# Two pre-norm attention layers on one core: another order for the first four and the last two phases

## The reference

```python
h = jnp.maximum(_layernorm(x, axis=-1), 0.0)
x = x + _L0_gnn_ref(h, adj, ...)   # q, k, v = h @ W + b per head
    # scores = q k^T / sqrt(32) + beta * adj; masked where adj <= 0; softmax; @ v
h = jnp.maximum(_layernorm(x, axis=-1), 0.0)
x = x + _L1_gnn_ref(h, adj, ...)   # q, k = h @ Wq.T, h @ Wk.T; v = h @ Wv.T + bv
    # a = q k^T * 384**-0.5 + adj; softmax; (a v) @ Wo.T + bo
return x
```

## Time and profile before

| | |
|---|---|
| median of 3 runs | 2226.38 us (2223.99 to 2227.64) |
| profiled execution | 2224.74 us |
| its span | 2222.9 us |
| granted TensorE clock, mean | 0.996 |
| PE busy | 97% of the span |
| ACT busy | 92% |
| DVE, POOL busy | 82%, 69% |

### The profile page before, as it was taken

The page is one execution under the profiler, slowest core; times in us unless marked ns, Lnnn a source line. Parts: engine busy times, 40 slices in busy tenths (PEclk is TensorE's granted clock), DMA queues, the critical chain, the costliest instruction groups (busy, mean ns, idle before and its releaser), DMA issues.

```text
span 2222.9 us, 75547 instructions
## 1 busy us (share of the span) xinstructions
PE 2160.5 (97%) x19968; PEld 1422.3 (64%) x19968; DVE 1820.4 (82%) x10186; ACT 2045.3 (92%) x7816; POOL 1530.5 (69%) x2439
## 2 busy tenths in 40 slices
PE   4999999999999999999999999999999999999997
PEld 1666666666666666665666666666666666666665
DVE  4788888888888888887888888888888888888777
ACT  3999999999999999998999999999999999999987
POOL 4567766767667767667676677676676776676665
PEclk9999999999999999999999999999999999999999
DMA  9787767778577677676676776676767867777861
GB/s 222 131 134 145 126 137 141 134 134 159 123 140 138 132 148 136 136 143 123 135 159 120 140 142 130 148 135 137 143 132 134 156 128 135 143 134 129 141 107 48
DMA packets 461311, 303.36 MB, mean 136 GB/s; under 512 B 228432, under 2 KB 460880, under 8 KB 460880
## 3 DMA queue, kind: packets, MB, share of 16 engines
q1 hardware_dynamic: 460880, 298.45, 70.8%
HBM read 71.83 MB, written 25.17 MB: 44 GB/s over the span
## 4 chain that ended last, share of the span: by engine, by line
PE 85%; DVE 7%; issue 3%; ACT 2%; POOL 1%; DMA 1%; SPq 0%; DVEq 0%; POOLq 0%; ACTq 0%
PE job_bank L909 47%; PE pt_bank L932 13%; PE o_bank L945 8%; PE score_bank L922 7%; PE inv_bank L968 3%; PE post_bank L978 2%; PE post_bank L982 2%; PE post_bank L979 2%; PE post_bank L960 2%; DVE neg L712 2%; ACT probs L606 1%; DVE part_lo L780 1%; DVE inv_wide L772 1%; DMA h<-h_rows 1%; DVE off_zero L763 1%
## 5 line engine op out<-in xcount | busy, mean ns | idle before, releaser
L606 ACT ACTIVATE probs<-neg,neg_max 128x128 f32<-128x128 f32 x3072 | 1189.7, 394 | 50.7 <-DVE neg_max L712 50.7
L909 PE MATMUL job_bank<-h,w_hi 128*128 128x512 f16 x2304 | 725.4, 381 | 29.6 <-DMA h<-h_rows 27.0
L606 ACT ACTIVATION_READ_ACCUMULATOR probs<-neg,neg_max 128x1 f32 x3072 | 595.2, 194 | 0.0
L631 ACT ACTIVATE probs_t<-pt_bank 128x512 f32<-128x512 f32 x768 | 450.0, 586 | 32.4 <-PE pt_bank L932 29.5
L932 PE MATMUL pt_bank<-ident,probs 128*128 128x128 f32 x3072 | 463.8, 274 | 10.8 <-ACT probs_t L631 10.0
L909 PE MATMUL job_bank<-h,w_lo 128*128 128x512 f16 x1152 | 438.2, 380 | 0.0
L932 PEld LDWEIGHTS pt_bank<-ident,probs 128*128 128x128 f32 x3072 | 366.0, 141 | 93.7 <-issue 13.1
L544 POOL TENSOR_TENSOR pair_sum<-neg 128x256 f32<-128x256 f32 x384 | 280.9, 732 | 197.7 <-DVE neg_max L712 183.6
L909 PE MATMUL job_bank<-w_hi,h 128*128 128x384 f16 x1536 | 413.6, 326 | 1.3 <-DVE part_lo L780 0.9
L712 DVE CUSTOM_DVE_ANT_0 neg<-score_bank,bias 128x128 f32<-128x128 f32 x1536 | 354.0, 286 | 28.5 <-issue 26.5
L712 DVE CUSTOM_DVE_ANT_0 neg<-score_bank,adj 128x128 f32<-128x128 f32 x1536 | 354.0, 285 | 14.1 <-issue 12.1
(11 more groups left out here) (65 smaller groups left out, 3513.1 us busy)
## 6 DMA issues: line engine op xcount, KB each, us to landing
stack<-part_hi SPq DMA_DIRECT2D x768, 128.0 KB, 3.5
stack<-part_lo SPq DMA_DIRECT2D x384, 128.0 KB, 3.8
x_res<-in_x SPq DMA_DIRECT2D x32, 768.0 KB, 5.8
out_x<-result_rows SPq DMA_DIRECT2D x128, 192.0 KB, 3.2
x_norm<-in_x SPq DMA_DIRECT2D x31, 768.0 KB, 6.0
adj<-in_adj SPq DMA_DIRECT2D x64, 256.0 KB, 3.8
h<-h_rows SPq DMA_TRANSPOSE x256, 3.9
probs_t<-in_x SPq DMA_DIRECT2D x1, 768.0 KB, 5.4
```

Source lines behind the costliest of these rows:

```text
L606: last = act.activation(probs[c % 2][:, h, :], neg[c % 2][:, h, :], ACT.Exp, bias=neg_max[:, b, first + h:first + h + 1], scale=-1.0, accu ...
L631: act.activation(probs_t[b % 2][:, first:first + HC, :].rearrange("p h q -> p (h q)"), pt_bank[:, :], ACT.Copy).then_inc(probs_t_ready, 1)
L909: last = pe.matmul(to, stationary, moving, start=(m == 0), stop=(m == MATMULS - 1))
```

## The change

It touches the first four phases and the last phases; the tables and the order inside the loop stay.

- **First loads.** x of the first group comes as four DMAs, two ahead of weight 0 and two behind it. Weight 2 comes behind the constants. `adj0` is issued after the first phase, `x_res` after the second. x of u1 is issued in slot 5 of the first phase instead of slot 4. x of u2 is issued in slot 10 of the second phase instead of the first.
- **Norm of u0 and u1** ("shared"): ACT writes the high part from `centred` (`high_rows`), DVE the low part (`low_rows`), POOL only `rstd`. There are four buffers for the centred rows and four for the split rows. The rows come in slots 0, 1, 2, 3 instead of 0, 2, 3, 5. For all units `shift_var` and `rstd` have four columns instead of two, and the waits for them are looser.
- **Second phase:** `PROJ_FIRST` leaves the first four slots without matmuls, then 11 per slot, then 12 in each of the last two.
- **Layer 1 weights:** loaded in slots 0, 3, 6 and 9 of the third phase, split by ACT in slots 3, 6, 9 of that phase and slot 0 of the fourth, and by DVE one slot later each. Their staging buffers are reordered, and POOL waits before it writes one.
- **Last unit:** its q and k jobs are spread over the phase that attends u62 (`PROJ_LAST_QK`), and its v jobs go into the phase that attends u63 itself (`PROJ_LAST_V`: 5 and 4 matmuls in two of every three slots).

```diff
+PROJ_FIRST = ((0, 0, 0),) * 4 + ((4, 4, 3),) * 6 + ((4, 4, 4),) * 2
+PROJ_LAST_QK = ((0, 4, 1), (1, 4, 0), (0, 4, 1), (4, 0, 1), (0, 4, 1), (5, 0, 1), (4, 1, 1), (2, 2, 1), (4, 4, 2),
+                (2, 0, 0), (0, 0, 0), (0, 0, 0))
+PROJ_LAST_V = ((0, 0, 5), (0, 0, 4), (0, 0, 0)) * GROUP
...
-HIGH_SLOTS = ({1: 0, 3: 1, 4: 2}, {4: 3, 6: 4, 8: 5, 10: 6})
-LOW_SLOTS = ({3: 0, 4: 1, 6: 2}, {5: 3, 7: 4, 9: 5, 11: 6})
+NORM_SLOTS_FIRST = (0, 1, 2, 3)
+SHARED_UNITS = 2
+LOW_ROWS_AT = (3, 0)
+LOAD_SLOTS = ({}, {}, {0: 3, 3: 4, 6: 5, 9: 6}, {})
+HIGH_SLOTS = ({2: 0, 3: 1, 5: 2}, {}, {3: 3, 6: 4, 9: 5}, {0: 6})
+LOW_SLOTS = ({4: 0, 6: 1, 8: 2}, {}, {4: 3, 7: 4, 10: 5}, {1: 6})
...
-        Phase(tail=u(n - 3), attend=u(n - 2), project=u(n - 1), look=u(n - 1)),
-        Phase(tail=u(n - 2), attend=u(n - 1), keep=kept(GROUPS - 1)),
+        Phase(tail=u(n - 3), attend=u(n - 2), project=u(n - 1), look=u(n - 1), table=PROJ_LAST_QK),
+        Phase(tail=u(n - 2), attend=u(n - 1), project=u(n - 1), keep=kept(GROUPS - 1), table=PROJ_LAST_V,
+              begin=QK_JOBS * MATMULS),
...
-            return (x_mid_bo[0], x_mid_bo[1], result_rows, x_mid)[m - 3][:, 0:KC, :]
+            return (x_mid, x_mid_bo[0], x_mid_bo[1], result_rows)[m - 3][:, 0:KC, :]
...
-            sp.dma_start(x_norm[:, :, :], x_groups[0]).then_inc(x_norm_in, 16)
+            def load_first(b):
+                sp.dma_start(x_norm[:, b, :], x[b]).then_inc(x_first_in[b], 16)
+
+            load_first(0)
+            load_first(1)
...
-            for m in range(3):
-                load_weight(m)
+            load_weight(0)
+            load_first(2)
+            load_first(3)
+            load_weight(1)
...
-            sp.dma_start(adj0[:, :, :], adj_groups[0]).then_inc(adj0_in, 16)
+            load_weight(2)
...
+                        if isinstance(g, int) and g < 2:
+
+                            if g == 1:
+                                sp.wait_ge(centred_ready, GROUP)
+                                sp.dma_start(x_norm[:, :, :], x_groups[2]).then_inc(x_norm_in, 16)
...
-                    if p.weights == 0 and s == 4:
+                    if p.weights == 0 and s == 5:
                         sp.dma_start(x_second, x_groups[1]).then_inc(x_second_in, 16)
+                    if p.weights is not None and s in LOAD_SLOTS[p.weights]:
+                        load_weight(LOAD_SLOTS[p.weights][s])
 
             phase(before()[0])
-            for m in range(3, WEIGHTS):
-                load_weight(m)
+            sp.dma_start(adj0[:, :, :], adj_groups[0]).then_inc(adj0_in, 16)
+            phase(before()[1])
             sp.dma_start(x_res[:, :, :], x_groups[0]).then_inc(x_res_in, 16)
-            run_phases(sp, phase, 1)
+            run_phases(sp, phase, 2)
...
+            def high_rows(u, b):
+                n = u.n * GROUP + b
+                act.wait_ge(rstd_done, n + 1)
+                act.wait_ge(centred_ready, n + 1)
+                if turned_before(u, b) > 0:
+                    act.wait_ge(h_in[b % 2], turned_before(u, b))
+                act.activation(rows_of(u, b)[:, 0, :], centred_of(u, b), ACT.Copy,
+                               scale=rstd[:, b:b + 1]).then_inc(h_high_ready, 1)
...
-                if some(n - 1):
-                    dve.wait_ge(h_rows_ready, n - 1)
+                if some(n - 3):
+                    dve.wait_ge(h_rows_ready, n - 3)
...
+            def low_rows(u, b):
+                n = u.n * GROUP + b
+                dve.wait_ge(h_high_ready, n + 1)
+
+                if n > 0:
+                    dve.wait_ge(h_rows_ready, n)
+                carry()
+                dve.scalar_tensor_tensor(rows_of(u, b)[:, 1, :], centred_of(u, b), rstd[:, b:b + 1],
+                                         rows_of(u, b)[:, 0, :], ALU.mult, ALU.subtract).then_inc(h_rows_ready, 1)
```

More of the change, by code:

```diff
@@ L134, in part @@
             return []
-        first = sum(sum(c) for c in self.counts()[:s]) + sum(self.counts()[s][:r])
+        first = self.begin + sum(sum(c) for c in self.counts()[:s]) + sum(self.counts()[s][:r])
         return [divmod(m, MATMULS) for m in range(first, first + self.counts()[s][r])]
@@ L153, in before @@
     return [
[L154 to L157, removed]
+        Phase(norm=u(0), weights=0, norm_slots=NORM_SLOTS_FIRST),
+        Phase(project=u(0), norm=u(1), look=u(0), bias=0, weights=1, table=PROJ_FIRST, norm_slots=NORM_SLOTS_FIRST),
+        Phase(attend=u(0), project=u(1), norm=u(2), look=u(1), bias=1, weights=2),
+        Phase(tail=u(0), attend=u(1), project=u(2), norm=u(3), look=u(2), bias=2, keep=kept(0), weights=3),
         Phase(tail=u(1), attend=u(2), project=u(3), norm=u(4), look=u(3), bias=3, keep=kept(1)),
@@ L229, in normed_in @@
 def normed_in(p, s, place, at):
-    if p.norm is None or place != at[1] or s - at[0] not in NORM_SLOTS:
+    if p.norm is None or place != at[1] or s - at[0] not in p.norm_slots:
         return None, 0
-    return p.norm, NORM_SLOTS.index(s - at[0])
+    return p.norm, p.norm_slots.index(s - at[0])
 def layer1_unit(group, off):
@@ L240, in layer1_unit, with shared @@
     return next(n for n in range(UNITS) if layer_and_group(n) == (1, group + off))
+def shared(u):
+    return isinstance(u.n, int) and u.n < SHARED_UNITS
 def chunk(u, c):
@@ L329, in build, with centred_of, rows_of, turned_before @@
         inv_bank = bank("inv_bank")
+        def centred_of(u, b):
+            if b < 2 or not shared(u):
+                return centred[b % 2][:, :]
+            return (o_rows, inv_wide)[b % 2][:, :, :].rearrange("p h d -> p (h d)")
+        def rows_of(u, b):
+            if b < 2 or not shared(u):
+                return h_rows[b % 2]
+            return (o_t, o_norm)[b % 2][:, :, :].rearrange("p c q -> p (c q)").bitcast(F16).rearrange(
+                "p (l d) -> p l d", l=2)
+        def turned_before(u, b):
+            if isinstance(u.n, int) and u.n < SHARED_UNITS:
+                return u.n * 32
+            return (u.n * 2 + b // 2) * 16
         def normed_rows(u, b):
@@ L344, in build @@
         w_lo_ready = sem("w_lo_ready")
+        x_first_in = [sem(f"x_first_in{b}") for b in range(GROUP)]
         x_norm_in = sem("x_norm_in")
@@ L649, in centre @@
                 act.wait_ge(shift_ready, n + 1)
[L651 removed]
+                if isinstance(u.n, int) and u.n < SHARED_UNITS:
+                    if u.n > 0:
+                        act.wait_ge(h_rows_ready, n - 3)
+                elif some(n - 1):
                     act.wait_ge(h_rows_ready, n - 1)
[L653 to L654 removed]
+                act.activation(centred_of(u, b), normed_rows(u, b), ACT.Relu,
+                               bias=shift_var[:, b, 0:1]).then_inc(centred_ready, 1)
+            def high_rows(u, b):
[6 more added lines that the diff above has]
+                               scale=rstd[:, b:b + 1]).then_inc(h_high_ready, 1)
             def phase(p):
```

66 lines of the change are left out of this document (38 added, 28 removed).

## The result

The changed kernel takes 2221.14 us (median of 22 runs, 2218.20 to 2225.37) against 2226.23 (22 runs, 2223.99 to 2229.08): ratio 0.9977, 95% interval 0.9971 to 0.9983. It is 5.1 us faster, where the prediction's sum gave 8.6 (2218). That lies inside the range of 2209 to 2224. The 0.2% that the prediction took as the least that can be told from no change is passed by 0.03%, and the interval has it inside, so the gain is clear of zero and not clear of 0.2%.

What follows compares the result with a forecast made beforehand. The prediction took DMA queues to bound the second phase and PE, with ACT close behind, from the fourth on. Front 8.0, less 2.7 for splits, plus 3.3 at the end gave 8.6 us less: median 2218, range 2209 to 2224.

Steps and rivals of the forecast that it cites:

- The bound at the start: First phase: DMA, not the split by ACT and DVE, becomes the limit; PE starts at 19.4 instead of 23.75 us.
- The stack stage: Second phase: DMA engines move 2.56 MB at 148 GB/s in 17.3 us; scores chunk 2 of u0 at 45.2 us.
- The new wait for x of u2: Start of third phase: DVE waits for this load and takes up chunk 2 of u0 2.4 us late.
- The front: Start to the first exponential of chunk 2 of u0: 8.0 us earlier, 58.54 to 50.5.
- The splits: Third and fourth phase: splitting layer 1's weights there costs 2.7 us, bounds 1.3 and 4.6.
- one of the prediction's signs of being wrong: Third phase: the prediction is wrong if ACT waits for a DMA there; no size given.
- rival 3: Third phase: ACT stands waiting for late weights, at 4.5 us each 9 us slower, 2236; chance 0.07.
- The clock at the head of the third phase: First matmuls there still run at 1.2 GHz; the price of about 2.3 us stays and cancels.
- The end: Last phases: moving u63's v matmuls into its own attended phase gains net 3.3 us (1 to 4.5).
- ACT becomes the bound, 3% on top: Phase that attends u62: PE falls to 29.4, ACT's 30.0 bounds it; 31.2 us, 4.3 less.
- it fits, barely, behind ACT: Last attended phase: PE's 20.1 us fit into 21.0 where ACT is busy 20.8; charged 1.0 (0 to 3).
- near 29 for its 28: Sign for the last attended phase: it should take near 29 us instead of 28.

Runs made afterwards that it cites:

- pool_split: The changed kernel with POOL splitting h of u0 and u1 again, two row buffers each; 2231.41 us, ratio 1.0023 to the kernel before.
- x2_first: The changed kernel with x of u1 issued behind the first transpose of u0, slot 3 instead of 5; 2217.68 us, ratio 0.9965 to the kernel before.
- x_early: The changed kernel with x of u2 and x_res issued ahead of the second phase; 2221.00 us, ratio 0.9977 to the kernel before.
- act_more: The changed kernel with one extra ACT instruction ahead of each high part of weights 3 to 6; 2224.13 us, ratio 0.9990 to the kernel before.
- w_second: The changed kernel with layer 1's weights loaded before and split in the second phase again; 2221.00 us, ratio 0.9978 to the kernel before.
- v_idle: The changed kernel with u63's v matmuls in blocks of nine at the first place of every third slot; 2219.26 us, ratio 0.9970.
- qk_even: The changed kernel with u63's q and k matmuls spread over slots 0 to 10 instead of 0 to 9; 2220.22 us, ratio 0.9971.
- pool_w: The changed kernel with GpSimd instead of ACT making the high parts of weights 3 to 6; 2219.42 us, ratio 0.9974 to the kernel before.
- inv_late: The changed kernel with ACT's copy of the turned inverse put behind the next slot's exponentials in the last three phases; 2221.95 us, ratio 0.9980.
- end_back: The changed kernel with the last unit's tables undone, all ten jobs of u63 in the phase that attends u62; 2223.14 us, ratio 0.9985.
- combo: The changed kernel with the edits of x2_first, v_idle, pool_w and x_early together; 2217.72 us, ratio 0.9963 to the kernel before.
- combo2: The changed kernel with the edits of x2_first, v_idle and pool_w together; 2215.02 us, ratio 0.9945 to the kernel before.

## Why the prediction was right, and where it was off

- **The bound at the start** (DMA queues ahead of the transposes and stacks) was half the story. The DMA engines are full to 21.5 us, but pool_split shows that what they are filled with, and when, hangs on the split of h, and x2_first that a single issue moves chunk 2 of u0 by 2.7 us. PE's start was put at 19.4 and is 21.58: 3.93 MB at 352 GB/s plus four transposes was too little. Of the four x blocks two stand behind weight 0, and DVE gets the third at 7.66 us. The first three transposes then hold SP for 1.85, 2.35 and 1.84 us, where the fourth takes 1.22, and so the x of u1 is issued only at 15.19. SP in the changed kernel:

```profile
8.86 4.33 SPq L518 DMA_TRANSPOSE h<-h_rows  x2
13.30 1.84 SPq L518 DMA_TRANSPOSE h<-o_t  x1
15.19 0.58 SPq L541 DMA_DIRECT2D probs_t<-in_x  x1
15.88 1.22 SPq L518 DMA_TRANSPOSE h<-o_norm  x1
```

  This error is 2.2 us, and it passes whole into the first stack (28.11 against 25.9).
- **The stack stage** was right in kind and mis-sized: 148 GB/s came from a stretch with faster loads at its head. Measured from the first stack to chunk 2 it is 21.1 us, not 19.3, so 1.8 us more. The Trainium skill, "SBUF — State Buffer", section "Door 1: The DMA port swizzle", says that a transfer on 32 partitions reaches 8 of the 16 ports and gives 189 GB/s measured at 1 MiB. These stacks write 32 partitions each; the trace agrees in the direction, as plain loads on 128 partitions flow at 352 GB/s, and not in the figure: the stage shows 133. The stacks are also smaller (128 KB each) and made of smaller packets than those loads, so no run shows that the partitions are the cause.
- **The new wait for x of u2** was right: predicted at 2.4 us, it cost 1.8 (x_early takes chunk 2 up at 49.88 instead of 51.68).
- **The front** in all: 8.0 forecast, 4.95 measured (58.54 to 53.59): 2.2 from PE's start and 1.8 from the stack stage, less what the wait for the x of u2 came out cheaper and the first exponential came sooner behind it.
- **The splits** were right: 2.7 forecast, 2.6 measured (64.28 to 66.86), and act_more shows that ACT's time counts there. The size is in part luck: against w_second, which has no splits in these phases, they cost 2.9 to 3.4 us, and w_second itself is 0.8 quicker than the kernel before. ACT waited 0.3 us once for a weight in the third phase. By the letter that is one of the prediction's signs of being wrong; in size it is nothing, and rival 3 did not come.
- **The clock at the head of the third phase** stays at 1.2 GHz in the changed kernel too: PEclk is 0.92 in that phase, 0.93 before, and every kernel here has 0.50 in the first 3 us from chunk 2 of u0. Here the Trainium skill, "TensorE: Matmul & The Clock Gate", Part 1, was right to speak against a gain: the array had idled 5.3 us.
- **The end** was off: 3.3 us forecast, and the two phases give 0.1 (1.6 less, 1.5 more). Two steps failed. "ACT becomes the bound, 3% on top" gave 31.2 us for a phase that takes 33.8. A part of it is PE's load: that fell by 4.3 us and not by 5.9 (35.33 to 31.02), since five of the v matmuls stand ahead of chunk 2 of u63; v_idle, which moves them, has 33.1. The rest is read from the rows of qk_even's passage and shown by no run: PE is full in some slots and ACT in others, so that neither's total is the bound; qk_even was to try this and was inconclusive. And "it fits, barely, behind ACT" counted PE's idle time without asking where it lies: the matmuls went into places where others waited behind them, 22.6 us where v_idle has 21.2. (The prediction's list of signs has "near 29 for its 28" for this phase, which fits none of its rows; its sum charges 1.0 on 21.0.) What I did not see pays in the profiled execution: its tail runs at 2.4 GHz (PEclk 1.00 against 0.85 before), 1.7 us shorter. That is not a gain to count on: of nine kernels with this table of v matmuls four have the full clock there.
- The rest of the 6.0 us between the two traces, 1.3 us, lies in the loop, from chunk 2 of u2 to that of u61: 1994.6 before, 1993.3 after. Other changed kernels show 1993.1 to 1994.9 there with the same code, so it cannot be told from chance.

Sum in the profiled executions, by the scores of chunk 2: u2 comes 2.7 us earlier (117.14 against 119.86), the loop gives 1.3, the phase that attends u61 0.2, the two phases behind it 0.1 and the tail 1.7, together 6.0. The medians differ by 5.1. So the terms that the prediction named gave 2.8 us of their 8.6, and 3.2 of the 6.0 came from the tail's clock, the loop and the phase before the end, which it had at nothing. That the median lies in the range owes something to that: with 2.8 alone it would be about 2223.4, near its edge at 2224. The range itself starts at 2209, below the 2211 of the prediction's own good ends.

## What to carry to other kernels

Idle time is only a place to put work if the slot in front of the idle engine's own wait is chosen: the same 36 matmuls made the last attended phase 1.5 us longer in one pair of places and 0.2 in another. Then look at the whole stretch to the end, since here the tail lost 1.7 us of that again. Where transfers queue, ask of each issue what stands behind its arrival on every in-order engine, before asking what bandwidth is left; one load two slots earlier brought chunk 2 of u0 forward by 2.7 us and the move of 2.36 MB gave nothing net. When an engine is relieved and the gain stays small, look for the wait that took its place, as in pool_w. A rate for a stage must be read from transfers of that stage's own shape.

## What the runs showed of the hardware

The clock at the end is not the same from kernel to kernel with the same end code. (Each kernel has one profiled execution.) Between the last two attended phases PE thins out, and in the profiled executions of x_early, w_second, pool_split and inv_late the granted clock fell there, while it held in the changed kernel, pool_w, x2_first and act_more. Busy time of x_early:

```profile
2144.10:2179.20 35.10, 32.30 (x296) 20.86 (x295) 25.96 (x146) 31.80 (x127) 18.91 (x30) 0.97 0.39 97
2179.20:2202.20 23.00, 19.57 (x208) 14.41 (x207) 17.85 (x103) 19.76 (x84) 16.09 (x24) 0.98 0.08 28
2174.00:2180.00 6.00, 4.21 (x28) 2.97 (x26) 5.13 (x31) 5.93 (x26) 3.83 (x6) 0.73 0.30 72
```

Where it fell, the end took 75.0 to 75.3 us, where it held 72.4 to 73.8; the kernel before took 74.3 and end_back 75.5. The tail behind chunk 11 of u63 varies by itself:

| profiled execution | v matmuls of u63 | tail, us | PEclk |
|---|---|---|---|
| changed, pool_w, x2_first, qk_even | 5 and 4 | 16.0 to 16.1 | 1.00 |
| act_more | 5 and 4 | 17.4 | 0.90 |
| x_early, w_second, pool_split, inv_late | 5 and 4 | 16.9 to 17.4 | 0.85 to 0.86 |
| v_idle, combo, combo2 | blocks of 9 | 17.4 to 17.8 | 0.85 to 0.87 |
| before, end_back | none | 17.8, 19.0 | 0.85, 0.79 |

With the same end code the tail is thus 16.0 us in one kernel's execution and 17.4 in another's, and the two places go apart: act_more kept the clock between the phases and lost it in the tail, qk_even the other way round. So the new end is worth 2 to 3 us in some executions and nothing in others. The changed kernel's single times go with its clock: of its 22 executions the eight with a mean granted clock of 0.998 took 2218.2 to 2221.0 us, the six with 0.996 took 2221.5 to 2225.4. Where in those executions the clock was lost is not on record.
